# Eight biases of the graph layers move from TensorE to GpSimd, and the first loads, the last unit's memory and the order of the program are laid out anew

## What is computed

```
x = layernorm(x + L0(x, adj))   # attention, 12 heads of 32, masked and biased by adj; q, k, v with biases
x = layernorm(x + L1(x, adj))   # two rounds: u = h.(hW)^T, exp, mask; ctx = attention @ (h W_lin + b_lin); norm, gain, relu
x = layernorm(x + L2(x, adj))   # two rounds: softmax(h h^T), mask; ctx = upper@(h Wl + bl) + diag*(h Ws + bs) + lower@(h Wr + br)
x = layernorm(x + L3(x, adj))   # attention, 12 heads, with adj as an additive term; v with bias, output projection Wo, bo
```

## Time and profile before

| | |
|---|---|
| time, median of 3 runs | 2942.34 us (2942.23 to 2944.7) |
| the profiled execution: its time, and its span from first to last instruction | 2937.27 us, 2935.5 us |
| PE busy | 2824.7 us (96%) |
| DVE, ACT, POOL busy | 2286.8 (78%), 1858.1 (63%), 1336.6 us (46%) |
| chain of waits, share by engine | PE 84%, DMA 7%, DVE 6% |
| L782, natural bias products | 576, of which 512 belong to the weights 5, 8, 9 to 14 |

### The profile page before, as it was taken

The page is one execution under the profiler, slowest core; times in us unless marked ns, Lnnn a source line. Parts: engine busy times, 40 slices in busy tenths (PEclk is TensorE's granted clock), DMA queues, the critical chain, the costliest instruction groups (busy, mean ns, idle before and its releaser), DMA issues.

```text
span 2935.5 us, 93395 instructions
## 1 busy us (share of the span) xinstructions
PE 2824.7 (96%) x35008; PEld 2091.3 (71%) x35008; DVE 2286.8 (78%) x8566; ACT 1858.1 (63%) x4885; POOL 1336.6 (46%) x2571
## 2 busy tenths in 40 slices
PE   4899999999999999999999999999999999999994
PEld 3666777777777777777777777777777777777762
DVE  5867787787787787787787787887787787887874
ACT  4655666666666666666666666666666666666653
POOL 1334454444444454454444454454454454444442
PEclk8899999999999999999999999999999999999997
DMA  6524444444454454444444454444444454454432
GB/s 172 122 47 70 79 86 74 78 86 76 77 87 76 76 87 73 78 87 76 77 88 74 79 87 75 80 83 75 82 83 77 79 85 75 78 87 78 73 61 52
DMA packets 803991, 237.41 MB, mean 81 GB/s; under 512 B 771544, under 2 KB 803416, under 8 KB 803424
## 3 DMA queue, kind: packets, MB, share of 16 engines
q1 hardware_dynamic: 796208, 218.87, 42.7%
q10 hardware_dynamic: 7344, 12.58, 1.4%
HBM read 29.99 MB, written 12.58 MB: 15 GB/s over the span
## 4 chain that ended last, share of the span: by engine, by line
PE 84%; DMA 7%; DVE 6%; ACT 1%; issue 1%; POOL 1%; SPq 1%; DVEq 0%; POOLq 0%; ACTq 0%
PE bank L776 11%; PE bank L777 10%; PE bank L778 10%; PE bank L764 9%; PE bank L765 8%; PE bank L766 8%; PE bank L868 7%; DMA turned<-flat 6%; PE bank L813 4%; PE bank L782 3%; PE bank L861 3%; PE bank L798 2%; PE bank L799 2%; PE bank L800 2%; PE bank L824 1%
## 5 line engine op out<-in xcount | busy, mean ns | idle before, releaser
L764 PE MATMUL bank<-turned,w_hi 128*128 128x128 f16 x4608 | 818.7, 221 | 10.9 <-DMA turned<-flat 7.6
L765 PE MATMUL bank<-turned,w_hi 128*128 128x128 f16 x4608 | 816.3, 220 | 0.0
L766 PE MATMUL bank<-turned,w_lo 128*128 128x128 f16 x4608 | 816.1, 220 | 0.0
L776 PE MATMUL bank<-w_hi,turned 128*128 128x384 f16 x2112 | 696.1, 330 | 34.8 <-DMA turned<-flat 33.8
L777 PE MATMUL bank<-w_lo,turned 128*128 128x384 f16 x2112 | 695.9, 330 | 0.0
L778 PE MATMUL bank<-w_hi,turned 128*128 128x384 f16 x2112 | 695.9, 329 | 0.0
L682 ACT ACTIVATE ab<-bank 128x384 f16<-128x384 f32 (+1 forms) x768 | 373.8, 487 | 304.3 <-PE bank L766 190.2
L691 ACT ACTIVATE score<-score,small 128x128 f32<-128x128 f32 x1536 | 500.9, 391 | 94.4 <-DVE small L951 91.7
L586 POOL TENSOR_TENSOR flat<-score,flat 128x384 f16<-128x384 f32 x256 | 234.5, 916 | 575.9 <-ACT flat L697 575.7
L764 PEld LDWEIGHTS bank<-turned,w_hi 128*128 128x128 f16 x4608 | 455.4, 99 | 47.6 <-DMA turned<-flat 15.9
L765 PEld LDWEIGHTS bank<-turned,w_hi 128*128 128x128 f16 x4608 | 452.8, 98 | 9.4 <-issue 1.6
(11 more groups left out here) (116 smaller groups left out, 6428.4 us busy)
## 6 DMA issues: line engine op xcount, KB each, us to landing
turned<-flat SPq DMA_TRANSPOSE x960, 2.8
x<-x_dram SPq DMA_DIRECT2D x64, 192.0 KB, 2.3
out_dram<-score SPq DMA_DIRECT2D x64, 192.0 KB, 2.3
w_stage<-w_dram ACTq DMA_DIRECT2D x18, 576.0 KB, 4.4
adj<-adj_dram SPq DMA_DIRECT2D x64, 64.0 KB, 2.2
rows<-rows_dram ACTq DMA_DIRECT2D x1, 1920.0 KB, 7.1
w_stage<-w_dram SPq DMA_DIRECT2D x1, 576.0 KB, 6.7
turned<-bias_dram SPq DMA_DIRECT2D x4, 9.0 KB
```

The costliest lines, as they stand in the source:

```text
L764: pe.matmul(dst, lhsT=w_hi[:, w, k, cols], rhs=t_hi[u][:, k, :], start=(k == 0), stop=False)
L765: pe.matmul(dst, lhsT=w_hi[:, w, k, cols], rhs=t_lo[u][:, k, :], start=False, stop=False)
L766: last = pe.matmul(dst, lhsT=w_lo[:, w, k, cols], rhs=t_hi[u][:, k, :], start=False, stop=(k == DT - 1 and w not in BIAS_OF))
L776: pe.matmul(dst, lhsT=t_hi[u][:, k, :], rhs=w_hi[:, w, k, :], start=(k == 0), stop=False)
```

## The change: what it does

1. The biases of weights 5, 8 and 9 to 14 leave PE. A new POOL part, "bias" w, waits for ACT "project" w and adds a row of rows to the result in place (128x384, full precision); PE "mix" waits for it (semaphore biased) and no longer for ACT. BIAS_OF keeps 0, 1 and 17.
2. rows has 18 rows where it had 10, and comes by two DMAs (8 rows, then 10), issued by ACT after its sixth and its fourteenth weight. bias_rows shrinks from three blocks to one.
3. The staging tiles of the weights lie in the memory of the unit with buffer number 6 (last_unit). Unit 6 is loaded only when all 19 weights are split; its columns of ones are written then. (In an order, last_unit stands for each tile of that unit.)
4. plan() treats the first loads, the weights and the two loads of rows as parts with dependences of their own; loads may go out 1.6 us apart (LOAD_EVERY), the three first weights are all loaded by ACT, and a transposition in the first 60 us counts as 1 us longer.
5. The table PARTS has new due times for every part (from 0 to 1094 where they went from 0 to 468), SHIFTED adds an offset to the due times of units 0 to 9 and 52 to 63, and PERIOD is 43.539. Some costs in the table differ too (scores on PE 0.36 for 0.28, the low parts on POOL 0.92 for 0.98, the issue of a transposition 1.24 for 1.35).

```diff
-BIAS_OF = {L0_Q: 0, L0_K: 1, 5: 2, 8: 3, 9: 4, 10: 5, 11: 6, 12: 7, 13: 8, 14: 9, L3_V: 10}
-NB = 3
-NR = 10
+BIAS_OF = {L0_Q: 0, L0_K: 1, L3_V: 2}
+NB = 1
+ROW_OF = {5: 6, 8: 7, **{w: 3 + w for w in range(9, 15)}}
+NR = 18
-PERIOD = 43.143
+PERIOD = 43.539
+SHIFTED = {0: -133.34, 1: -34.85, 2: -13.30, 3: -1.44, 4: -27.85, 5: -68.55, 6: -35.55, 7: -24.78, 8: 13.07, 9: 2.79, 52: -0.24, 53: 3.39, 54: 55.93, 55: 32.10, 56: 104.09, 57: 153.04, 58: 149.72, 59: 189.33, 60: 138.03, 61: 18.06, 62: 37.42, 63: -195.00}
...
-    (PE, "mix", 0): (155.20, 0.700, 0.830, ((SCALAR, "project", 5), (VECTOR, "delta_gcn", 0)), ()),
+    (PE, "mix", 0): (428.38, 0.700, 0.830, ((POOL, "bias", 5), (VECTOR, "delta_gcn", 0)), ()),
+    (POOL, "bias", 5): (532.73, 0.920, 1.050, ((SCALAR, "project", 5),), ()),
...
-WEIGHTS_FROM, WEIGHT_EVERY, LOAD_EVERY = 5.5, 4.4, 10.0
+ROWS_AFTER, ROWS_SPLIT = (5, 13), 8
+LOAD_FROM, LOAD_EVERY, BETA_AT = 2.2, 1.6, 9.0
+CROWDED = 60.0
...
+            wanted[part, i] = i * PERIOD + SHIFTED.get(i, 0.0) + at
...
+    for i in range(UNITS - 1):
+        soonest[(SYNC, "load", 0), i] = LOAD_FROM + LOAD_EVERY * i - (0.9 if i else 0.0)
+    comes_after(((SYNC, "load", 0), UNITS - 1), ((VECTOR, "weight", WEIGHT_ORDER[-1]), 0))
...
+        if part in TRANSPOSES and now < CROWDED:
+            until += 1.0
...
-        w_stage = [sb(f"w_stage_{slot}", [128, DT * D])[:, :] for slot in range(STAGES)]
+        w_stage = [last_unit[:, n * DT * D:(n + 1) * DT * D] for n in range(STAGES)]
...
             def load(i, k):
+                if i == UNITS - 1:
+                    sp.wait_ge(w_lo_made, NW)
...
+            def bias(i, w):
+                u = i % UNITS
+                pool.wait_ge(*proj_hi_done.at(i, "made", w))
+                if (w, i) == first(POOL, "bias", 5, 8):
+                    pool.wait_ge(rows_loaded[0], 16)
+                if (w, i) == first(POOL, "bias", *range(9, 15)):
+                    pool.wait_ge(rows_loaded[1], 16)
+                made = proj[u][2 if w < 9 else (w - 9) % 3]
+                pool.tensor_tensor(made, made, rows[:, ROW_OF[w], :], ALU.add).then_inc(biased.of(i), 1)
...
             def attend(i, s):
                 pe.wait_ge(*landed.at(i, "p", s))
+                if (s, i) == (0, UNITS - 1):
+                    pe.wait_ge(last_unit_ready, 3)
...
             def mix(i, k):
-                    pe.wait_ge(*proj_hi_done.at(i, "made", L1_W[k][2]))
+                    pe.wait_ge(*biased.at(i, "made", L1_W[k][2]))
...
                     for w in L2_W[k - 2]:
-                        pe.wait_ge(*proj_hi_done.at(i, "made", w))
+                        pe.wait_ge(*biased.at(i, "made", w))
```

More of the change, by code:

```diff
@@ new lines @@
+    (PE, "mix", 1): (90.17, 0.700, 0.830, ((POOL, "bias", 8), (VECTOR, "delta_gcn", 1)), ()),
+    (PE, "attend", 0): (148.98, 0.234, 0.454, ((SYNC, "scores", 0),), ()),
+    (POOL, "inner", 1): (166.58, 0.570, 0.693, ((VECTOR, "inner", 1),), ()),
+    (PE, "u_gcn", 0): (186.29, 1.012, 1.192, ((VECTOR, "project", 3), (VECTOR, "project", 4)), ()),
+    (VECTOR, "divide", 0): (192.17, 0.800, 0.966, ((SCALAR, "attend", 3),), ()),
+    (SCALAR, "turn", 0): (208.47, 0.470, 0.641, ((SYNC, "load", 0),), ()),
@@ new lines, in plan @@
+    for i in range(B):
+        for part, (at, _, _, after, after_last) in PARTS.items():
+            wanted[part, i] = i * PERIOD + SHIFTED.get(i, 0.0) + at
+            comes_after((part, i), *((p, i) for p in after))
+            if i >= UNITS:
+                comes_after((part, i), *((p, i - UNITS) for p in after_last))
+        for w in WEIGHT_ORDER:
+            comes_after(((PE, "project", w), i), ((VECTOR, "weight", w), 0))
+            if w in BIAS_OF:
+                comes_after(((PE, "project", w), i), ((VECTOR, "biases", 0), 0))
+        comes_after(((POOL, "bias_x", 0), i), ((SCALAR, "load_rows", 0), 0))
+        for k in range(4):
+            comes_after(((VECTOR, "inner", k), i), ((SCALAR, "load_rows", k // 2), 0))
+        for w in ROW_OF:
+            comes_after(((POOL, "bias", w), i), ((SCALAR, "load_rows", 0 if w < 9 else 1), 0))
@@ L639, in _ @@
         def _(act):
-            for n in (1, 2):
+            for n in range(STAGES):
                 load_weight(act, n)
```

528 lines of the change are left out of this document (271 added, 257 removed).

## The result

The changed kernel takes 2977.61 us in the median of 4 runs (2976.61 to 2984.79), the kernel before 2942.28 on the same chip (4 runs, 2937.92 to 2944.7). The ratio is 1.0132, 95% interval [1.0118, 1.0146]: it is slower by 35 us, where 99 less were forecast. The profiled execution took 2978.49 us.

The account below looks back on a forecast made before the run. PE was taken to bound the middle, 43.9 us a unit. 2937.27 - 76 + 9 - 18 - 14 = 2838.3 us profiled, with 5.07 a median of 2843; forecast 2815 to 2865 (0.55), 8 in 10 from 2800 to 2890.

Parts of the forecast that it names:

- The shared read interface, priced at 0: DVE and GpSimd reading SBUF: meetings add 1.0 us a unit, DVE 35.1 to 36.1, under 42.6, so 0 in the sum.
- The rule: Skill's statement: two-SBUF-input DVE and SBUF-reading GpSimd instructions exclude each other, the later waiting for the whole earlier one; speaks against the change.
- Rival D: DVE becomes the bound: all 15 two-input instructions of a unit meet GpSimd, 45.8 us a unit, +110, 3050 us; chance 0.05.
- The bias products, -76: Eight of nine bias products leave PE at L782, 1.30 us a unit: -76 us, bounds -83.5 and -62.
- The wait on GpSimd, +9: Mix on PE now waits behind ACT's copy and a POOL addition: 0.15 us a unit over 58 units, +9 us.
- rival C: Wait moves to mix: two of four mixes a unit find their bias late, 40 us; 2874 or 2906 us; chance 0.12.
- The ends, -18 and -14: Start (67 us lost) gives back 18, bounds -40 and +5; end (60 us lost) gives 14, bounds -35 and +10.
- A: The ends give nothing, as weights come at the DMA's pace and the end is a chain: 2875 us; chance 0.13.
- B: The ends give most of their bounds, -30 and -25, and no new waits: 2811 us; chance 0.12.
- E: The removal is no gain because PE's bias products were covered: 2942 us; chance 0.03.
- The prediction's own sign of being wrong: A unit in the middle takes 43.5 us or more, or the end costs more than 60 us.

Follow-up runs that it names:

- e2_memset: Changed kernel with each of the eight GpSimd bias additions replaced by two memsets of the same tile, waits kept: 2856.49 us, ratio 0.9717.
- e1_no_adds: Changed kernel without the eight GpSimd bias additions, mix waiting for ACT's copy, queue order kept: 2852.73 us, ratio 0.9701.
- e9_searched_on: Changed kernel, all eight additions kept, order planned with GpSimd/DVE exclusion and due times from a longer search: 2921.13 us, ratio 0.9942.
- e8_one_input: Changed kernel with each of the eight bias additions replaced by a one-input GpSimd instruction adding constant 0.5 in place: 2881.65 us, ratio 0.9806.
- e6_four_adds: Changed kernel with the additions of weights 5, 9, 11, 13 kept and those of 8, 10, 12, 14 left out: 2924.62 us, ratio 0.9955.
- e5_same_order_pe: Changed kernel with the eight biases back as PE products, every queue in exactly the changed kernel's order: 2913.24 us, ratio 0.9911.

## Why the prediction was wrong

The forecast was 2843, faster; it became 2978, slower. By the steps of the prediction:

- **The shared read interface, priced at 0: this is the step that failed.** It put DVE at 36.1 us a unit, and took this to be free because it is under 42.6. DVE became 40.7 and a unit 45.0, and the term is 121 us (changed kernel against e2_memset). Two things in it were wrong.

  *What it costs.* With 121 us for 64 x 8 additions that read, one addition costs 0.24 us of the end time, without DVE being full. The sum does not decide it: e1_no_adds has 2.6 us more of DVE in a unit than before and loses nothing by them. How much of the 121 us the additions would cost without these 2.6 us is open; in the order of e9_searched_on they cost 32.

  *What meets what.* The medians of the earlier trace rows were read as a sign that meetings are rare whatever the order is. Comparing start times in the middle of the two traces, for eight kinds of DVE instructions (the fifteen two-input ones of a unit, and the two of the masks): before, 41 of 697 began inside a GpSimd instruction on a 128x384 tile, all of them L971 with some 0.12 us of a low part left, at no cost; after, 267 of 679 do, 6.7 a unit, and they are longer by 4.1 us a unit. The medians told of that order and not of the hardware. Of the 267, 203 met one of the eleven low parts and row additions of a unit that POOL had already (L1111 inside L628 and L633, 59 times in 160); the forecast left these out. It counted the meetings of the fifteen with the new additions alone, 2.9 a unit and 1.0 us, and for these the 1.0 us is met, by luck: they are 1.6 a unit and each is dearer. It also left out other instructions that meet the additions, for 1.5 us a unit: the 128x128 sums L1055 and L1060 and L1036, with one input, above all.
- **The rule.** The Trainium skill ("SBUF — State Buffer", on who interferes with whom) says that the two kinds exclude each other and that the later waits for the whole of the earlier; it spoke against the change and was given 1 us a unit. The two-input additions did what it says (L1030, 580 ns longer with 745 to come), and writes alone do not contend, as it also says (e2_memset). The same page names a DVE instruction with one input in a two-port mode among those that contend; L989, one input, went from 217 to 720 ns, by meetings with the low part L622. Where a one-input instruction of GpSimd reads SBUF, e8_one_input differs from the rule (held up to 0.35 of its 1.2 us), and the measurement decides.
- **Rival D** had the right mechanism and side, with the wrong condition. It was to decide from 7.5 us more of DVE in a unit, when DVE fills it, and to be slower from 8.8. It was slower at 5.7 more (3.1 of them by the additions), with DVE busy 90% of the stretch. The waits of PE in 600 to 2400 us, before and then after (total us, times, longest), say why:

```profile
PE bank L764 <- DMA turned<-flat: 5.8, 10, 1.2
PE bank L824 <- DMA turned<-flat: 1.2, 4, 0.5
```

```profile
PE bank L824 <- DVE score L1097: 23.2, 30, 1.0
PE bank L858 <- DVE ab L1003: 13.9, 31, 0.6
PE bank L923 <- DVE score L1060: 11.8, 30, 0.4
```

  PE waited for no DVE instruction before. Now it does, mostly at these three kinds of places, 1.0 us at most each time; such waits are 61 of the 77 us that PE is idle there. Queues in order need room for every instruction, not in the sum of a unit. e6_four_adds says the same: with four additions DVE has 5 us to spare in a unit, and PE waits all the same.
- **The bias products, -76 (bounds -83.5 and -62).** e5_same_order_pe against e1_no_adds measures -60.5, just outside the bounds: in the middle 43.8 to 42.7 us a unit, 1.1 for the 1.30 that the timeline gave.
- **The wait on GpSimd, +9 (bounds -4 and +230).** It is 4 us, from e1_no_adds to e2_memset. Mix's lines wait for POOL 3.4 us in the whole program, under 15 as forecast. So rival C is out.
- **The ends, -18 and -14.** The order, first loads and ends together bring 26 us with the biases on PE (e5_same_order_pe against before), for 32. The end saved 12 (forecast 14). The last low half of a weight is made at 82.5 us (117.2 in the earlier trace rows; forecast before 95); POOL's wait for rows is 14.1 us and not under 10, and it costs little, because the six low parts are ahead of it; but the DMA engines are 95% busy in the first 60 us (60% in the earlier trace rows), and between 60 and 118 us PE makes 547 matmuls for 662: it waits 11.3 us there for transpositions, 8.9 of them at once, and its clock falls. That the new loads are the cause is likely and not shown. The work of the first 250 us is worth 4.66 x 43.9 = 205 us, as forecast. Rivals A, B and E are out.

The prediction's own sign of being wrong, a unit of 43.5 us or more, came with 45.0. Without the reads the sum is nearly right: e2_memset, which has everything else, took 2856 for the 2843 forecast. Of the 135 us that are missing 121 lie in one term; the bias products, the ends and the wait on GpSimd are off by 16, 6 and -5 us.

## What to carry to other kernels

A median that shows no contention shows what one order does. Before work with two SBUF inputs goes to GpSimd beside a DVE that is busy 80% of the time, count how often the instructions of both overlap in the new order, the old work of GpSimd included, and price each meeting at what is left of the GpSimd instruction, half a microsecond and more here, even if DVE's sum stays under the bound. And due times found for one set of parts don't serve another: after moving work, plan anew with the contention in the costs.

## What the runs showed of the hardware

- A GpSimd addition with two SBUF inputs (1000 ns) holds up a two-input DVE instruction that begins inside it until it ends: L1030, 40 times, 580 ns more in the mean with 745 of the addition left. Small ones are held as well: L1060 (128x128) 39 times, 497 ns more with 628 left.
- One-input DVE instructions between SBUF tiles can be held too: L1036 (128x12) 38 times, 538 ns more with 673 left; L989 (128x128) inside the low part L622 31 times, 645 ns more with 785 left.
- GpSimd writes (two of 417 ns) don't hold up the two-input kinds (e2_memset). A one-input GpSimd instruction of 1177 ns holds up two-input DVE instructions only in its beginning: 256 ns more for 71 that began in its first 0.3 us, 5 ns for 257 that began later.
- DVE instructions with their first input in PSUM (L1003, 549 ns) keep their length inside two-input additions: 37 times inside L643, 2 ns more.
- TensorE's granted clock was 0.74 from 60 to 118 us. It was 0.50 (1.2 GHz) from 70 to 95 us, where PE had been busy 2.5 of the 10 us before, and 1.00 (2.4 GHz) from 100 us on, where it had been busy 8.7 of the 10 us before. In the middle it was 1.00, though PE waited 77 of 1800 us there, none of its waits being over 1.4 us.
